# Second attention phase of a four-phase transformer kernel: value projections in four parts, a new order of its tasks, and row transfers issued by SyncE

## The reference

```python
    q = (x @ Wq.T + bq).reshape(b, l, h, hd).transpose(0, 2, 1, 3)
    k = (x @ Wk.T + bk).reshape(b, l, h, hd).transpose(0, 2, 1, 3)
    v = (x @ Wv.T + bv).reshape(b, l, h, hd).transpose(0, 2, 1, 3)
    scores = jnp.einsum('bhqd,bhkd->bhqk', q, k) / math.sqrt(hd)
    scores = jnp.where(causal, scores, -jnp.inf)
    att = jax.nn.softmax(scores, axis=-1)
    out = jnp.einsum('bhqk,bhkd->bhqd', att, v)
    out = out.transpose(0, 2, 1, 3).reshape(b, l, d)
    return out @ Wo.T + bo
...
    x = x + _L0_attn_b_ref(_layernorm(x, axis=-1), ...)
```

## Time and profile before

| | |
|---|---|
| median of 3 runs | 1942.3 us (1941.38 to 1946.25) |
| the profiled execution, its own time | 1948.8 us |
| its span from first to last instruction | 1947.0 us |
| granted TensorE clock, mean | 0.935 |
| PE / PE weight loads / DVE / ACT / POOL busy | 86% / 60% / 56% / 44% / 33% |
| bytes moved | 106.96 MB, 55 GB/s |

### The profile page before, as it was taken

How to read it: one execution, slowest core, us unless ns; L and a number is a source line. 1 busy time by engine, 2 the same in 40 slices (tenths; PEclk the granted TensorE clock), 3 DMA queues, 4 the chain that set the end, 5 groups by cost and what they waited for, 6 DMA issues and landing times. The chain is left out here.

```text
span 1947.0 us, 31527 instructions
## 1 busy us (share of the span) xinstructions
PE 1669.1 (86%) x10544; PEld 1159.5 (60%) x10544; DVE 1099.4 (56%) x2394; ACT 864.5 (44%) x1514; POOL 647.5 (33%) x1926
## 2 busy tenths in 40 slices
PE   5888989889976999999279798799889857999997
PEld 4555655566544787777255465465456435787785
DVE  5777677776726654543445645654644527655543
ACT  3456555555524544533224443443443415454541
POOL 4455455454421321311224433433443412221211
PEclk8899999999986999999679999999899988999999
DMA  2000000000016311010432423423343226211010
GB/s 99 2 19 18 35 24 15 33 2 29 19 44 187 101 65 40 25 43 17 146 51 47 76 45 69 79 51 66 59 64 66 46 67 173 94 52 65 0 44 22
DMA packets 78119, 106.96 MB, mean 55 GB/s; under 512 B 13194, under 2 KB 49674, under 8 KB 77972
## 3 DMA queue, kind: packets, MB, share of 16 engines
q1 hardware_dynamic: 76271, 104.71, 21.4%
q10 hardware_dynamic: 1701, 0.39, 0.1%
HBM read 62.34 MB, written 16.78 MB: 41 GB/s over the span
## 5 line engine op out<-in xcount | busy, mean ns | idle before, releaser
L247 PE MATMUL f_ring<-f_xt,f_codes 128*128 128x512 f32 (+1 forms) x1408 | 360.7, 399 | 6.3 <-DVEq L1548 5.3
L247 PEld LDWEIGHTS f_ring<-f_xt,f_codes 128*128 128x128 f32 (+1 forms) x1408 | 264.0, 188 | 76.0 <-DVEq L1548 6.1
L1406 POOL TENSOR_TENSOR f_ht<-f_work,f_ht 128x512 fp32r<-128x512 f32 (+1 forms) x88 | 114.5, 1305 | 473.4 <-ACT f_ht L1466 473.4
L841 ACT ACTIVATE ab_region<-ab_scores 128x512 f32<-128x512 f32 x320 | 184.0, 600 | 100.5 <-PE ab_scores L1131 92.2
L841 ACT ACTIVATE aa_region<-aa_scores 128x512 f32<-128x512 f32 x320 | 184.1, 599 | 80.1 <-PE aa_scores L1131 77.2
L698 POOL TENSOR_SCALAR_AFFINE_SELECT ab_region<-ab_region 128x128 f32<-128x128 f32 x512 | 138.6, 294 | 208.6 <-ACT ab_region L841 207.9
L1559 DVE TENSOR_TENSOR f_work<-f_ring,f_work 128x512 f32<-128x512 f32 (+1 forms) x176 | 120.6, 690 | 146.0 <-ACT f_work L1455 117.2
L1455 ACT ACTIVATE f_work<-f_ring,f_scales 128x512 f32<-128x512 f32 (+1 forms) x176 | 120.5, 685 | 171.8 <-PE f_ring L247 171.3
L247 PE MATMUL f_ring<-f_dcodes,f_ht 128*128 128x512 f32 (+1 forms) x704 | 175.8, 404 | 10.3 <-DVE f_down_x L1529 9.3
L1131 PE MATMUL ab_scores<-ab_stacks 99*128 99x512 bf16 (+3 forms) x512 | 130.1, 318 | 47.8 <-DMA ab_stacks<-ab_rowparts 45.5
L698 POOL TENSOR_SCALAR_AFFINE_SELECT aa_region<-aa_region 128x128 f32<-128x128 f32 x512 | 136.5, 295 | 91.0 <-ACT aa_region L841 90.5
(11 more groups left out here) (181 smaller groups left out, 2980.5 us busy)
## 6 DMA issues: line engine op xcount, KB each, us to landing
ab_stacks<-ab_parted SPq DMA_DIRECT2D x192, 128.0 KB, 4.1
f_x<-mid SPq DMA_DIRECT2D x32, 256.0 KB, 3.8
f_raw<-mid SPq DMA_DIRECT2D x32, 256.0 KB, 4.1
f_raw<-in_gate_q SPq DMA_DIRECT2D x10, 512.0 KB, 5.4
f_raw<-in_up_q SPq DMA_DIRECT2D x10, 512.0 KB, 4.9
f_raw<-in_down_q SPq DMA_DIRECT2D x10, 512.0 KB, 3.6
aa_x<-in_x SPq DMA_DIRECT2D x16, 256.0 KB, 2.8
aa_res<-in_x SPq DMA_DIRECT2D x16, 256.0 KB, 2.8
```

The costliest lines, as they stand in the source:

```text
L247: mm = pe.matmul(out, w, x, start=start and i == 0, stop=stop and i == len(pairs) - 1)
L841: act.activation(probs[:, s // 2 % 2, SUB * (s % 2) + i, :], scores[:, sbk, :], ACT.Exp, scale=0.25).then_inc(scores_freed[sbk].sem, 1)
L1406: pool.tensor_tensor(ht[0:r, LO, n, :], hid[0:r, n % 2, :], ht[0:r, HI, n, :].bitcast(F32), ALU.subtract).then_inc(hid_lo.sem, 1)
```

## The change

Only phase `ab` is reordered. Five things change.

1. `project_values` does two units and two blocks of 128 tokens at a time: 24 matmuls of 256 columns and 4 bias matmuls. There are still four V tasks in a batch, now (unit pair, half of the tokens). Those of units 0 and 1 for the next batch are done at slots 65 and 71 of this one, those of units 2 and 3 at slots 5 and 28 of their own; ScalarE copies each out in two instructions.
2. The output projections of the batch before, in slots 14 to 17, go to 12, 22, 31 and 35. The context transposes C, in slots 33, 53, 73 and 93 (13 of the next batch), go to 48, 69, 74 and 89 (9).
3. The projection of queries for unit 1 moves from slot 0 to slot 78 of the batch before, K of unit 1 from 2 to 0; the S pieces of unit 1 get the same slots as those of the others (0, 0, 1, 1, 3, 3, 4, 4, 5, 5, 6, 6 from the unit's start). X goes from 46, 48, 53, 56 to 43, 46, 51, 54.
4. SyncE issues all rows of `ab` at the start of slot i=2, as in `aa`. ScalarE issues none.
5. The head's cut is at slot 40 instead of 20, and `EARLY_B` adds what has no batch before it.

```diff
@@ Timetable, sync, scalar
-        self.cut = self.SUB * (7 if units == 2 else 4)
+        self.cut = self.SUB * (7 if units == 2 else 8)
...
-                        if rope and i == ROWS_AT and (after := following(region, b0 + bs, s, 1)) is not None:
-                            max_rows(sp, *after)
+                        if i == ROWS_AT and (after := following(region, b0 + bs, s, 1)) is not None:
+                            max_rows(*after)
...
-                        src = banks.read(act, where, ("V", 0, t, 0)).rearrange("p (n h d) -> p n h d", n=QUADS, d=HD)
-                        act.wait_ge(av_made.sem, av_made.at(b0 + bb, 0))
-                        act.copy(v[:, :, t, :, 0:HD], src).then_inc(banks.is_free(where, ("V", 0, t, 0)), 1)
+                        src = banks.read(act, where, ("V", u, t, 0)).rearrange("p (a q h d) -> p a q h d", a=2, q=QPU * 2, d=HD)
+                        act.wait_ge(av_made.sem, av_made.at(b0 + bb, 2 * QPU * (u - 1)))
+                        quads = slice(2 * QPU * u, 2 * QPU * (u + 1))
+                        for a in range(2):
+                            last = act.copy(v[:, quads, 2 * t + a, :, 0:HD], src[:, a])
+                        last.then_inc(banks.is_free(where, ("V", u, t, 0)), 1)
...
-                        if not rope and i == ROWS_AT + 1 and (after := following(region, b, s, 1)) is not None:
-                            max_rows(act, *after)
@@ tensor
+            def project_values(out, g, half):
+
+                units_of = lambda ap: ap.rearrange("p (u n) -> p u n", n=NU)[:, 2 * g:2 * g + 2, NQ + NKV:NU]
+                for a in range(2):
+                    t, at = 2 * half + a, 2 * NKV * a
+                    tok = slice(t * P, (t + 1) * P)
+                    passes(pe, out[:, at:at + 2 * NKV], [(xt[:, x_part, f, tok], units_of(w[:, c, f, 0:OO]))
+                                                         for f in range(KD) for x_part, c in THREE], stop=False)
+                    for k in range(2):
+                        mm = passes(pe, out[:, at + k * NKV:at + (k + 1) * NKV],
+                                    [(sel[:, 2 * g + k, :], bias[:, NQ + NKV:NU])], start=False, stop=k == 1)
...
@@ PLAN_B
-    (0, "Q", 0, 1, 0), (2, "K", 0, 1, 0),
...
-    *[(j, "V", 0, 0, t) for t, j in enumerate((5, 7, 9, 11))],
-    *late(17, 10, "F"), *late(33, 20, "C"),
-    *[(j, "O", -1, 0, t) for t, j in enumerate((14, 15, 16, 17))],
-    *[(j, "X", 1, 0, t) for t, j in enumerate((46, 48, 53, 56))],
...
+    (78, "Q", 1, 1, 0), (0, "K", 0, 1, 0), (18, "Q", 0, 2, 0), (20, "K", 0, 2, 0), (37, "Q", 0, 3, 0),
...
+    (5, "V", 0, 1, 0), (28, "V", 0, 1, 1), (65, "V", 1, 0, 0), (71, "V", 1, 0, 1),
+    *late(17, 10, "F"),
+    (48, "C", 0, 0, 0), (69, "C", 0, 0, 1), (74, "C", 0, 0, 2), (9, "C", -1, 0, 3),
+    *[(j, "O", -1, 0, t) for t, j in enumerate((12, 22, 31, 35))],
+    *[(j, "X", 1, 0, t) for t, j in enumerate((43, 46, 51, 54))],
 )
+EARLY_B = timed((0, "Q", 0, 1, 0), (3, "V", 0, 0, 0), (7, "V", 0, 0, 1))
```

More of the change, by code:

```diff
@@ L263, with __init__ @@
     SUB = 5
-    def __init__(self, units, plan, head, n_parts):
+    def __init__(self, units, plan, head, n_parts, early):
         self.units, self.n_parts = units, n_parts
-        self.cut = self.SUB * (7 if units == 2 else 4)
+        self.cut = self.SUB * (7 if units == 2 else 8)
         end = self.SUB * PAIRS
@@ L272, in __init__ @@
         self.head = ([None] * pure + line(0, 0, self.cut), dict(head))
-        self.head[1].update({pure + j: [(k, bb, u, t) for k, bb, u, t in plan.get(j, []) if bb == 0]
+        self.head[1].update({pure + j: early.get(j, []) + [(k, bb, u, t) for k, bb, u, t in plan.get(j, []) if bb == 0]
                              for j in range(self.cut)})
@@ L359, in is_free, with attention @@
         return self.freed[self._at(where, use)[0]]
-def attention(nc, phase, name, consts, x_dram, y_dram, w_dram, kv_heads, units, plan, head,
+def attention(nc, phase, name, consts, x_dram, y_dram, w_dram, kv_heads, units, plan, head, early,
               rope_dram=None, bias_dram=None, biassel_dram=None):
@@ L385, in attention @@
     MAXIMA, TASKS = 3, 2
-    table = Timetable(units, plan, head, TPARTS)
+    table = Timetable(units, plan, head, TPARTS, early)
     HI, LO = 0, 1
@@ L607, in _, with max_rows @@
                 load(1, t)
+            def max_rows(b, s):
+                sp.wait_ge(rows_copied.sem, rows_copied.at(b, s + 1))
+                h, _, _ = heads(s, 0)
+                sp.dma_start(stacks[MAXROW:MAXROW + 3, unit(s) % 2, h:h + 2, :],
+                             rowparts[MAXROW:MAXROW + 24, :]).then_inc(rows_made.sem, 16)
             def residual(b, t):
@@ L630, in part @@
                     for n, (_, bb, u, t) in enumerate(table.started(region, pos, 0, "S")):
-                        if n == 0:
+                        if n == 0 and b0 + bs + s + i > 0:
                             scores_seen(b0 + bs, SUB * s + i - 1)
@@ L1077, in project_rows @@
                 return passes(pe, out, pairs)
-            def project_values(out, t):
-                tok = slice(t * P, (t + 1) * P)
-                cols = lambda c, f: w[:, c, f, 0:OO].rearrange("p (u n) -> p u n", n=NU)[:, :, NQ + NKV:NU]
-                passes(pe, out, [(xt[:, x_part, f, tok], cols(c, f)) for f in range(KD) for x_part, c in THREE],
-                       stop=False)
-                for u in range(units):
-                    mm = passes(pe, out[:, u * NKV:(u + 1) * NKV], [(sel[:, u, :], bias[:, NQ + NKV:NU])],
-                                start=False, stop=u == units - 1)
+            def project_values(out, g, half):
[8 more added lines that the diff above has]
+                                    [(sel[:, 2 * g + k, :], bias[:, NQ + NKV:NU])], start=False, stop=k == 1)
                 return mm
@@ L1139, in values @@
                     pe.wait_ge(rows_copied.sem, rows_copied.at(b, 2 * n + 4))
-                if not rope and n == 0:
-                    banks.all_emptied(pe, where, [("V", 0, t, 0) for t in range(NT)])
+                if not rope and n % (2 * QPU) == 0:
+                    made_in = ("body", b - 1) if b else ("head", 0)
+                    banks.all_emptied(pe, made_in, [("V", n // (2 * QPU), k, 0) for k in range(2)])
                 pe.wait_ge(cut_off.sem, cut_off.at(b, 2 * SUB * (n + 1)))
@@ L1166, in transposes @@
                 else:
-                    banks.emptied(pe, where, ("F", 0, 2 * t + 1, 0))
+                    earlier = ("body", b - 1) if b else ("head", 0)
+                    banks.emptied(pe, where if rope or t else earlier, ("F", 0, 2 * t + 1, 0))
                 for i in range(NT):
@@ L1209, in part @@
                         elif kind == "V":
-                            out = banks.take(pe, where, ("V", 0, t, 0))
-                            project_values(out, t).then_inc(banks.is_filled(where, ("V", 0, t, 0)), 1)
+                            out = banks.take(pe, where, ("V", u, t, 0))
+                            if region is table.head:
+                                pe.wait_ge(w_lo_made, 1 + KD)
+                            project_values(out, u, t).then_inc(banks.is_filled(where, ("V", u, t, 0)), 1)
                         elif kind == "P":
@@ L1703, in program @@
         with Phase(nc) as phase:
-            attention(nc, phase, "aa", consts, d["x"], mid[0], d["wa"], KV_GQA, UNITS_A, PLAN_A, HEAD_A,
+            attention(nc, phase, "aa", consts, d["x"], mid[0], d["wa"], KV_GQA, UNITS_A, PLAN_A, HEAD_A, {},
                       rope_dram=d["trig"])
@@ L1708, in program @@
         with Phase(nc) as phase:
[L1709 removed]
+            attention(nc, phase, "ab", consts, mid[1], mid[2], d["wb"], HEADS, UNITS_B, PLAN_B, HEAD_B, EARLY_B,
                       bias_dram=d["bias"], biassel_dram=d["biassel"])
```

16 lines of the change are left out of this document (4 added, 12 removed).

## The result

| | before | after |
|---|---|---|
| median | 1945.2 us (1941.38 to 1954.77, 7 runs) | 1929.45 us (1926.12 to 1935.66, 7 runs) |
| ratio, 95% interval | 1 | 0.9918 [0.9894, 0.9942] |
| the profiled execution | 1948.8 us | 1928.0 us |
| phase `ab`, first score matmul of batch 0 to the last step | 574.4 us | 555.1 us |

The kernel is faster by 0.8%, some 16 us, where 43 were forecast (from 1942.3 to 1899). The time lies just inside the range, which is owed to the range's width. The change worked as a change and yielded little more than a third of its forecast. In the experiments one execution, of the new plan alone, took 4049 us; it counts in that kernel's median and not in its ratio.

The account below looks back on a forecast made before the run. TensorE and its waits, chiefly for rows, were taken to bound the kernel. Rows -39.5, other idle +5, clock -12, V +4 sum to -42.5 us: 1948.8 to 1906.3, less 6.5 for the median, 1899 us; range 1876 to 1930.

Parts of the forecast that it names:

- What bounds the kernel: Phase ab: TensorE and its waits set the length; 70.7 us idle, 45.5 of it for rows, and 25.4 from low clock.
- K steps, step 3, bare steps: Steps with a K projection and step 3 stop waiting for rows; four steps without a task late in batch 3 keep 0.4.
- Steps 1, 5, 9, 13 at 0.3 us each: Odd steps whose rows stand behind pieces issued in slots 5 and 6: 0.3 us of wait left in each of 15.
- land by 16.8: Pieces of slots 3 to 6 arrive 16.8 us from the unit's start, needed at 16.1; costed at nothing, bound 8 us.
- Rival A: Pieces still hold rows up: K steps keep 1.2 to 1.8 us, 22 us in all, total 1926 us; chance 0.12.
- Cover in the odd steps: Any 3 us task in slots 2 to 4 of an odd step covers its wait for the rows.
- a path of 2.6 us: Time from transposes to score matmul with SyncE issuing, against 2.2 us of TensorE work in an odd step without a task.
- Other idle time: TensorE's 25.2 us of idle not for rows: 2 less for X tasks, 7 more for VectorE and GpSimd, net +5 us.
- Low clock: TensorE's reduced clock in phase ab costs 25.4 us; at 0.97 of full clock 12 us are saved, bounds 5 and 21.
- V matmuls: Value projections in halves: 256-column matmuls at 0.130 us, 0.26 us more in each of 16 tasks, +4 us.
- rival D: Value matmuls not in proportion to their columns: +118 us in place of +4, 2013 us; with other losses chance 0.07.
- ScalarE and SyncE: ScalarE's 62 fewer issues and 16 more copies cost nothing; SyncE's 16 more issues a batch likewise, with delayed pieces bounded at 8.

Follow-up runs that it names:

- the new plan alone: The changed kernel with ScalarE issuing the rows again, in slot i=3 behind its exponential: 1932.6 us, 0.9945 of the kernel before.
- Small pieces: The changed kernel with query and key pieces of 64 tokens instead of 512, sent to a buffer nothing reads: 1904.5 us, 0.9796 of the kernel before.
- V later: The changed kernel with three value projections moved behind their step's transposes, from slots 5, 65, 71 to 8, 68, 73: 1932.9 us, 0.9938 of the kernel before.
- the queries first: The changed kernel with all six query pieces sent ahead of the K step's rows, key pieces in slots 3, 3 and 4: 1909.0 us, 0.9809 of the kernel before.

## Why the prediction was right or wrong

- **What bounds the kernel**: right. Small pieces gave 25 us for the rows' waits and the clock behind them.
- **K steps, step 3, bare steps**: right. Rows in K steps took 1.9 to 2.0 us (2.04 forecast) and no K step but the very first waits for them; step 3 doesn't wait (its 1.15 are gone); of the bare steps late in batch 3, only step 11 waits, 0.36 where four at 0.4 were forecast.
- **Steps 1, 5, 9, 13 at 0.3 us each**: this step failed, 4.5 us forecast and 22.6 measured. I saw the pieces of slots 3 to 6 go out behind the rows, worked out that they "land by 16.8", and used that only for the matmuls that read the pieces. The rows of the next step queue behind the same pieces. I also took the 4.57 us of the earlier trace rows, which is the rows' own flight behind pieces, for that of the last of eight pieces; issued one every 0.64 us, they land 1.06 to 1.1 us apart and are done at 18.3. And I looked at the residual load's wait for its store only as something that rows could stand behind; the last four pieces of step 5 stood behind it. Rival A had the pieces' mechanism but put it in the wrong steps, in the K steps behind the first four, and "the pieces of slots 5 and 6 stand ahead of them" only in a half sentence; its 22 us of waits and 1926 us come close to what happened.
- **Cover in the odd steps**: the list of tasks is right (C in steps 1, 9 and 13, V in step 5, all behind the transposes), and it was measured against a path of 2.6 us. Against rows that land at 18.4 to 19.7 neither is enough. The V tasks in slots 5 and 65 stand ahead of the transposes; V later showed that this costs nothing by itself.
- **Other idle time**: +5 forecast, 53.9 - 24.0 = 29.9 against 25.2, +4.7. That this fits is luck: the parts were -2 for X and +7 for the rest, and measured are +1.3 (11.9 for 10.6) and +3.4.
- **Low clock**: 12 us forecast. By the windows 2 x (141.03 x 0.04 + 147.29 x 0.05 + 146.54 x 0.05 + 120.20 x 0.03) = 47.9 us at the lower level, for 60.6: 12.7 x 0.42 = 5.3 us. I had assumed a clock of 0.97 for waits that would be gone. Each batch keeps a drop or two in steps 8 to 10, and batches 1 to 3 have one just behind the 2.2 us wait of step 1, which in batch 1 ends at 1150.50:

```profile
1152.70:1156.10 3.40, 3.40 (x11) 2.62 (x10) 0.57 (x2) 0.23 (x1) 0.64 (x3) 0.50 0.01 2
1227.80:1234.60 6.80, 6.09 (x27) 2.89 (x31) 5.64 (x14) 2.28 (x4) 3.89 (x14) 0.50 0.12 39
```

  With the queries first the drops of batches 1 to 3 behind step 1 are gone and those of steps 8 to 10 stay.
- **V matmuls**: +4 forecast, +1.8 measured, with 0.120 us from one start to the next where 0.130 was forecast; rival D has no ground.
- **ScalarE and SyncE**: nothing forecast for ScalarE, right. SyncE's 16 more issues cost nothing as issues; what they cost is the pause in front of them, which holds the pieces back. The prediction saw the pieces wait, asked only for the matmuls that read them, and put it at nothing (bound 8).

Sum of the measured terms: -21.5 (rows) + 4.7 - 5.3 + 1.8 = -20.3 us, where the phase is 19.3 us shorter and the profiled executions differ by 20.8; the medians differ by 16. (The forecast's own sum ends at 1899.8, recorded as 1899.) Of the 42.5 in the forecast 18.0 went in the steps behind K steps and 6.7 in the clock, and 2.5 came in elsewhere. Most of the first and a part of the second come back when two more pieces leave ahead of the pause, at 1909 us.

## What to carry to other kernels

A small DMA on a path that sets the end landed here about when the large ones issued ahead of it had landed, so follow every large transfer to its landing, at its pace and not at its latency, and ask which later small one it meets. An instruction that makes a queue wait delayed all that stood behind it, eight pieces behind the rows and four behind a residual load: put what is ready ahead of it. And cover counts only against a landing that the cover does not itself move; moving work behind an early issue gains nothing while bytes fix the arrival.

## What the runs showed of the hardware

A first piece of 128 KB (one DMA, SBUF to SBUF) took 3.3 us and each further one in a row 1.06 us more, 122 GB/s with all 16 DMA engines shown busy; the row transfer took 1.9 to 2.0 us on either queue without company, and up to 6.0 us on SyncE's with six pieces in flight. With V later, rows that ScalarE issued for the step behind a K step landed no earlier than SyncE's own in some steps and 0.7 to 1.3 us earlier in others, 18.2 us from the K step's start at the earliest. TensorE's fp32 matmuls of 256 columns in the V tasks started 0.12 us apart (median), and those of 512 columns 0.23, so the narrow ones are only 4% dearer per column.
